# Two groups moved from DMA to TensorE transposes, DMA issues shifted between two queues, and one load issued by another engine

## The chip, the cores and the metric

One core of one Trainium2 chip (trn2) runs the whole kernel. The metric is the device time of one launch in microseconds (us); lower is better. A time is given as the median of several executions, and one execution was recorded by the hardware profiler, which is where every row below comes from.

## What is computed

The reference is one transformer block on 2048 tokens of width 128, all in float32. `mod` (six vectors of 128) is made from `c`.

```python
h = layernorm(x) * (1 + ca) + sa
q, k, v = h @ w_qkv                      # 16 heads of 64
a = softmax(causal(q k^T / 8)) v         # 2048 x 2048 per head
x = x + ga * (a @ w_out)
h = layernorm(x) * (1 + cb) + sb
e = argmax(h @ Wr.T + br)                # one of 8 experts for each token
x = x + gb * (relu(h @ W1[e].T + b1[e]) @ W2[e].T + b2[e])
```

## The kernel before

**Attention.** The 16 heads are taken as 8 pairs. A pair has 8 groups g = 0..7 of 256 queries; group g sees 2g+2 key tiles of 128 (`tiles_of`). In a group a row r = 0..3 is 128 queries of one head. TensorE (PE) makes the scores into a ring of four PSUM banks (L899). VectorE (DVE) copies them to `probs` with the row maximum (L1286, L1289, L1293). ScalarE (ACT) takes the exponential in place (L1129). Before probabilities can be multiplied by v they must be transposed, and this is done in two ways:

- *Turned on PE.* For tile j, PE transposes the four 128x128 blocks into one of three PSUM banks (L912, a "turn"), and ACT (L1137) or DVE (L1322) copies that bank to one of five slots `pT` (a "take"). The first turn of a group waits until all four rows have been through the exponential.
- *Moved by DMA.* The first `far(g)` tiles of groups 3 to 7 (4, 4, 5, 5, 5 tiles). DVE transposes within 32x32 squares into `staged` (L1303, a "shuffle", one for each row r), and small DMAs between partitions in SBUF put the squares in place in `turned_far`. Half u = 0 are rows 0 and 1, half u = 1 rows 2 and 3. A half has 16 DMAs, by a source block a = 0..3 and a target block b = 0..3. `move_blocks` (L641 to L651) issues the four of one (u, a). In the kernel before, the sync queue (SP) issues a = 0, 1 and GpSimd (POOL) issues a = 2, 3 of each half. The 8 pairs have 40 moved groups.

Then PE multiplies the turned tiles by v (L940, a "pv", one for each tile). `pv_order` puts the turned tiles first and the moved ones last. The first moved tile waits until all 32 DMAs of the group have landed. A shuffle of half u waits until the DMAs of that half of the moved group before have landed, as `staged` has one buffer.

**The order of the work.** `Plan` simulates PE, ACT and DVE step by step with written-down costs (`took`) and ready times (`ready`), and writes out one fixed order for each engine. Moves have a modelled time in `move_at`: start, then eight issues of `ISSUE` = 650 ns, then `LAND` = 4200 ns. The SP queue's order comes from `transfers`: moves, the round trip of the row sums through DRAM (L699 "put", L710 "get", which `norm` L1339 needs), weights, and the blank rows of the sorted buffer (L728). The POOL order holds moves and the copies of k to the other half of the partitions (L795). Each queue is strictly in order.

**The end.** In the last pair, as tokens are finished, PE, DVE and ACT also do the residual, the second layer norm and the routing for five parts of the tokens (4, 4, 4, 2, 2 tiles: L953, L963, L1357 to L1421, L978 to L1012). POOL scatters the rows of each tile to the sorted buffer (L803, `scatter(i)`). SP loads W2 (L693) after the last turn of group 6, and W1 (L685) and the broadcast of b2 (L686) after the last score. POOL, after `scatter(0)` to `scatter(3)`, places b1 (L813), waits for b2 and multiplies it by the gate (L818), fills small tables in the space of `staged` (L823 to L828), and issues `scatter(4)`. DVE needs these tables for `ends` (L1427), and the gated b2 before its first copy of an expert (L1458). PE turns W1 and W2 after the last pv (L1036, L1039). A loop over 23 tiles sorted by expert follows.

Of the kernel before, what the change touches and what calls it, by code (L numbers as in the profile page):

```python
# [24 lines left out]
FAR_BUFS = 2  # L25
ISSUE = 650.0
LAND = 4200.0
# [33 lines left out]
def far(g):  # L61

    return FAR.get(g, 0)


def pv_order(g):

    return list(range(far(g), tiles_of(g))) + list(range(far(g)))
# [32 lines left out]
class Plan:  # L101
# [9 lines left out]
    def __init__(self):  # L111
        groups = [(p, g) for p in range(PAIRS) for g in range(GROUPS)]
        scores = [(p, g, r, c) for p, g in groups for r in range(4) for c in range(chunks(g))]
        turns = [(p, g, j) for p, g in groups for j in range(far(g), tiles_of(g))]
        pvs = [(p, g, j) for p, g in groups for j in pv_order(g)]
        self.moves = [(p, g) for p, g in groups if far(g)]
# [43 lines left out]
        for m, (p, g) in enumerate(self.moves):  # L160
            steps += [(self.move_at(m, u)[0] + 4 * ISSUE * i, "move", (p, g, u, 2 + i)) for u in range(2) for i in range(2)]
# [19 lines left out]
    def ready(self, kind, key):  # L181
# [8 lines left out]
        if kind == "pv":  # L190
            free = 0.0
            if key[2] == pv_order(g)[0] and p + g and min(groups_of(*self.part_of(p, g))) == g:
                free = at("norm", *self.part_of(*group_before(p, g)))
            return max(self.turned_at(key), at("value", p, key[2] // 4), free)
# [7 lines left out]
        if kind == "proj":  # L202

            last = (("score", p - 1, 2 * g + 1, 3, chunks(2 * g + 1) - 1), ("score", p - 1, GROUPS - 1, 3, g),
                    ("pv", p - 1, GROUPS - 1, max(range(4 * g, 4 * g + 4), key=pv_order(GROUPS - 1).index)))[key[2]]
            return max(self.ring_free(), at(*last) if p else 0.0)
        if kind == "top":
            past = group_before(p, g, 2)
            k0, w = piece(g, key[2], key[3])
            behind = 0.0  # L210
            if past and k0 < tiles_of(past[1]) * P:
                behind = at("shuffle", past[0], past[1], key[2]) if far(past[1]) else 0.0
                over = min((k0 + w) // P, tiles_of(past[1])) - 1
                if over >= far(past[1]):
                    behind = max(behind, at("turn", past[0], past[1], over))
            return max(at("score", *key), behind)
# [7 lines left out]
        if kind == "norm":  # L224
            last = groups_of(p, g)[-1]
            i = p * CHUNKS + min(g, CHUNKS - 1) - 2
            return max([self.got(p, last), at("pv", p, last, pv_order(last)[-1])] +
# [9 lines left out]
        if kind == "wturn":  # L237
            free = max(at("pv", p, GROUPS - 1, pv_order(GROUPS - 1)[-1]),
# [14 lines left out]
    def move_at(self, m, u):  # L253

        if (m, u) not in self.moved:
            p, g = self.moves[m]
            begin = max(self.at("shuffle", p, g, 2 * u + r) for r in range(2))
            if m >= FAR_BUFS:
                q, f = self.moves[m - FAR_BUFS]
                begin = max(begin, self.at("pv", q, f, far(f) - 1))  # L260
            if u or m:
                begin = max(begin, self.move_at(m if u else m - 1, 1 - u)[0] + 8 * ISSUE)
            if begin >= NEVER:
                return NEVER, NEVER
            self.moved[m, u] = begin + HOP, begin + HOP + 8 * ISSUE + LAND
        return self.moved[m, u]

    def turned_at(self, key):

        p, g, j = key  # L270
        return self.move_at(self.move_no[p, g], 1)[1] if j < far(g) else self.at("take", *key)
# [8 lines left out]
    def transfers(self):  # L280
# [12 lines left out]
        for m, (p, g) in enumerate(self.moves):  # L293
            for u in range(2):
                for a in range(2):
# [4 lines left out]
                          self.at("shuffle", p, g - 1, 3) if far(g - 1) else 0.0) + HOP, "w2", (p,)))  # L300
# [17 lines left out]
    def took(self, kind, key, engine):  # L318
# [17 lines left out]
        if kind == "shuffle":  # L336
            return far(key[1]) * P / 0.96 + 100.0
# [43 lines left out]
    def choose_pe(self, now, soon):  # L381
# [11 lines left out]
        turn_at = place("turn", lambda k: (k[2] - far(k[1])) / float(tiles_of(k[1]) - far(k[1])))  # L393
# [23 lines left out]
def adaln_block(nc, x, w_qkv, w_out, Wr, br, W1, b1, W2, b2, c_in, wmod, out):  # L417
# [27 lines left out]
    with ExitStack() as ctx:  # L445
# [195 lines left out]
        def move_blocks(queue, key, landed):  # L641
# [4 lines left out]
            if m >= FAR_BUFS:  # L646
                q, f = plan.moves[m - FAR_BUFS]
                queue.wait_ge(pv_done, plan.order[q, f, far(f) - 1] + 1)
            for b in range(P // SQUARE):
                queue.dma_start(turned_far[b * SQUARE:(b + 1) * SQUARE, m % FAR_BUFS, u, a, 0:far(g), :],  # L650
                                staged[a * SQUARE:(a + 1) * SQUARE, u, b, 0:far(g), :]).then_inc(landed[u], 16)  # L651
# [4 lines left out]
        def _(sp):  # L656
# [21 lines left out]
            for s in plan.sp:  # L678
# [3 lines left out]
                elif s.kind == "w1":  # L682
# [3 lines left out]
                    sp.dma_start(experts[:, :, B2_AT:W2_AT],  # L686
                                 b2.rearrange("(a e) d -> a e d", a=1).broadcast_to([P, NE, E])).then_inc(b2_in, 16)
                elif s.kind == "w2":

                    sp.wait_ge(rows_turned, plan.number[p, GROUPS - 2, tiles_of(GROUPS - 2) - 1] + 1)  # L690
                    if far(GROUPS - 2):
# [38 lines left out]
            for u in range(2):  # L730
                sp.wait_ge(moved[u], 128 * len(plan.moves))
                sp.wait_ge(moved_soft[u], 128 * len(plan.moves))
# [19 lines left out]
        def _(pool):  # L752
# [59 lines left out]
            pool.wait_ge(bank_free[b_bank], b_use + 1)  # L812
            nc.gpsimd.tensor_copy(experts[:, :, B1_AT:B2_AT],  # L813
# [26 lines left out]
        def _(pe):  # L840
# [26 lines left out]
            for s in plan.pe:  # L867
# [34 lines left out]
                elif s.kind == "turn":  # L902
# [3 lines left out]
                    if j == far(g):  # L906
# [8 lines left out]
                elif s.kind == "pv":  # L915
                    j = s.key[2]
                    first, last = pv_order(g)[0], pv_order(g)[-1]
# [10 lines left out]
                    if j < far(g):  # L928
                        m_no = plan.move_no[p, g]
                        if j == 0:  # L930
                            for u in range(2):
                                pe.wait_ge(moved[u], 128 * m_no + 128)
                                pe.wait_ge(moved_soft[u], 128 * m_no + 128)
# [246 lines left out]
        def _(dve):  # L1180
# [69 lines left out]
            for s in plan.dve:  # L1250
# [17 lines left out]
                elif s.kind == "top":  # L1268
# [6 lines left out]
                    if past and far(past[1]) and c == 0:  # L1275

                        dve.wait_ge(shuffled, 4 * plan.move_no[past] + r + 1)
                    if past and k0 < tiles_of(past[1]) * P and (r == 0 or (r == 2 and c == n - 1)):

                        over = min((k0 + w) // P, tiles_of(past[1])) - 1  # L1280
                        if over >= far(past[1]):
# [13 lines left out]
                elif s.kind == "shuffle":  # L1295
# [4 lines left out]
                    if m and h == 0:  # L1300
                        dve.wait_ge(moved[u], 128 * m)
                        dve.wait_ge(moved_soft[u], 128 * m)
                    dve.transpose(staged[:, u, :, 0:far(g), h * SQUARE:(h + 1) * SQUARE],  # L1303
                                  probs[g % 2][:, r, 0:far(g) * P].rearrange("p (j b i) -> p b j i", j=far(g), i=SQUARE)
# [19 lines left out]
                elif s.kind == "norm":  # L1324
# [3 lines left out]
                    dve.wait_ge(pv_done, plan.order[p, last, pv_order(last)[-1]] + 1)  # L1328
# [190 lines left out]
```

## Time and profile before

| what | us |
|---|---|
| median of 3 executions | 979.15 |
| these executions | 978.80, 984.84, 979.15 |
| the profiled execution, its own time | 988.01 |
| its span in the profile | 986.3 |
| busy in that span: PE, DVE, ACT, POOL | 913.3, 761.9, 633.8, 422.6 |

A row of the profile names engine and line ("PE L912"), what it writes and reads (`out<-in`), how many instructions are merged (x8), when it started and how long it took, and in brackets how long the engine had been idle and what released it. SPq is the sync queue; its rows are issues of DMAs, not transfers.

### The profile page before, as it was taken

To read this page: it belongs to the slowest core of one execution; us is meant where nothing else is said; L and a number is where in the kernel's file an instruction comes from. 1 tells how busy PE (TensorE), PEld (TensorE's weight loads), DVE (VectorE), ACT (ScalarE), POOL (GpSimd) and SP (SyncE) were. 2 spreads that over 40 slices of the span, in tenths; PEclk is the share of its full clock that TensorE was granted. 3 is DMA by queue.
4 is the path that set the end of the run, shared out by engine and by line. 5 is a ranking of instruction groups with operands and counts; after the bars stand their busy time and mean duration, and the time that the engine had idled before them with its cause. 6 is when DMAs were issued, how large, how long until landed. Compare 5 with 4: busy or idle time off the path is not lost.

```text
span 986.3 us, 19842 instructions
## 1 busy us (share of the span) xinstructions
PE 913.3 (93%) x6115; PEld 674.7 (68%) x6115; DVE 761.9 (77%) x2426; ACT 633.8 (64%) x1158; POOL 422.6 (43%) x765
## 2 busy tenths in 40 slices
PE   4999999989998999899998999899989999995796
PEld 3776767667675767677676767676767666773796
DVE  6898869875997769785988599867978689971463
ACT  4876668656774768665865677577857566551574
POOL 0274515442364316542554236431745144445054
PEclk9899999999999999999999999999999999986898
DMA  2035312342144302531245214430343013372120
GB/s 81 12 91 133 100 38 64 104 125 66 29 111 109 92 23 79 136 99 47 56 106 131 66 30 113 111 95 22 88 118 87 20 47 84 87 226 69 31 67 18
DMA packets 107211, 79.13 MB, mean 80 GB/s; under 512 B 32935, under 2 KB 94163, under 8 KB 107106
## 3 DMA queue, kind: packets, MB, share of 16 engines
q1 hardware_dynamic: 85378, 51.57, 19.7%
q0 software_dynamic: 21728, 26.29, 10.2%
q8 instruction: 50, 0.82, 0.4%
q14 instruction: 55, 0.45, 0.2%
HBM read 18.21 MB, written 11.77 MB: 30 GB/s over the span
## 4 chain that ended last, share of the span: by engine, by line
PE 59%; SPq 16%; DVE 12%; issue 5%; DMA 4%; ACT 2%; another core or an unknown queue 1%; POOL 1%; POOLq 0%; DVEq 0%; ACTq 0%
PE ps L940 18%; PE ps L899 13%; SPq L650 12%; PE ps L912 12%; PE ps L878 4%; DVE probs L1286 4%; DMA turned_far<-staged 3%; PE ps L882 3%; PE ps L1064 2%; DVE probs L1289 2%; PE ps L1075 2%; PE ps L953 2%; SPq L710 2%; SPq L699 2%; DVE staged L1303 1%
## 5 line engine op out<-in xcount | busy, mean ns | idle before, releaser
L650 POOL DMA_DIRECT2D turned_far<-staged x640 | 313.1, 497 | 353.4 <-DVE staged L1303 340.4
L1129 ACT ACTIVATE probs<-probs,neg_max 128x128 f32<-128x128 f32 (+15 forms) x256 | 308.7, 1207 | 151.2 <-DVE neg_max L1293 148.6
L899 PE MATMUL ps<-k_both,q_both 128*128 128x512 f32 (+2 forms) x1280 | 344.1, 393 | 12.9 <-DVE probs L1286 7.7
L899 PEld LDWEIGHTS ps<-k_both,q_both 128*128 128x128 f32 x1280 | 208.7, 190 | 84.9 <-issue 30.5
L1286 DVE TENSOR_SCALAR_CACHE_REDUCE probs<-ps 128x512 f32<-128x512 f32 (+1 forms) x384 | 243.4, 662 | 5.0 <-PE ps L899 4.0
L1137 ACT COPY pT<-ps 128x512 f32<-128x512 f32 (+1 forms) x341 | 177.1, 557 | 94.8 <-PE ps L912 76.3
L912 PE MATMUL ps<-ident,probs 128*128 128x128 f32 x1440 | 203.8, 278 | 2.3 <-ACT probs L1129 1.4
L912 PEld LDWEIGHTS ps<-ident,probs 128*128 128x128 f32 x1440 | 172.4, 143 | 46.5 <-issue 23.3
L940 PE MATMUL ps<-pT,v_sb 128*64 128x256 f32 (+1 forms) x1568 | 179.1, 370 | 5.7 <-DVE pT L1322 3.8
L940 PEld LDWEIGHTS ps<-pT,v_sb 128*64 128x64 f32 x1568 | 104.4, 137 | 74.0 <-issue 19.1
L1303 DVE STREAM_TRANSPOSE staged<-probs 128x640 f32<-128x640 f32 (+1 forms) x160 | 122.0, 778 | 37.6 <-DMA turned_far<-staged 15.9
L1289 DVE CUSTOM_DVE_ANT_0 probs<-ps,causal 128x256 f32<-128x256 f32 (+3 forms) x256 | 130.2, 509 | 8.1 <-PE ps L899 7.8
L795 POOL CAST k_both<-k_both 64x1024 fp32r<-64x1024 f32 x64 | 66.4, 1037 | 148.2 <-DVE k_both L1265 145.6
L940 PE MATMUL ps<-turned_far,v_sb 128*64 128x256 f32 x736 | 93.0, 400 | 17.8 <-DMA turned_far<-staged 17.8
L940 PEld LDWEIGHTS ps<-turned_far,v_sb 128*64 128x64 f32 x736 | 56.1, 143 | 43.0 <-issue 24.3
L878 PE MATMUL ps<-hT,w_pair 128*128 128x512 f32 x128 | 63.4, 599 | 0.2 <-DVE q_both L1261 0.2
L1261 DVE SCALAR_TENSOR_TENSOR q_both<-ps,q_both 64x512 fp32r<-64x512 f32 x64 | 44.1, 689 | 20.9 <-ACT q_both L1115 19.7
L1322 DVE COPY pT<-ps 128x512 f32<-128x512 f32 (+1 forms) x51 | 31.5, 617 | 30.0 <-PE ps L912 15.1
L1339 DVE TENSOR_TENSOR oT<-ps,rinv_b 128x512 f32<-128x512 f32 (+1 forms) x33 | 22.1, 670 | 41.7 <-PE ps L940 40.7
L1129 ACT ACTIVATION_READ_ACCUMULATOR probs<-probs,neg_max 128x1 f32 x256 | 48.8, 190 | 0.0
L1265 DVE TENSOR_TENSOR k_both<-ps,k_both 64x512 fp32r<-64x512 f32 x64 | 44.1, 689 | 5.7 <-ACT k_both L1115 4.5
L1293 DVE TENSOR_REDUCE neg_max<-row_max 128x1 f32<-128x1 f32 (+3 forms) x256 | 39.8, 155 | 8.9
(147 smaller groups left out, 700.7 us busy)
## 6 DMA issues: line engine op xcount, KB each, us to landing
turned_far<-staged POOLq DMA_DIRECT2D x384, 40.0 KB, 2.5
turned_far<-staged SPq DMA_DIRECT2D x384, 40.0 KB, 2.0
x_sorted<-blank SPq DMA_DIRECT2D x19, 458.5 KB, 5.3
rinv_b<-spread_rows SPq DMA_DIRECT2D x128, 64.0 KB, 2.7
turned_far<-staged SPq DMA_DIRECT2D x256, 32.0 KB, 1.9
turned_far<-staged POOLq DMA_DIRECT2D x256, 32.0 KB, 1.8
spread_rows<-rinv_rows SPq DMA_DIRECT2D x256, 0.5 KB
probs<-in_L_ffn_W_dram SPq DMA_DIRECT2D x1, 2048.0 KB, 11.6
```

The source lines that it names most:

```text
L650: queue.dma_start(turned_far[b * SQUARE:(b + 1) * SQUARE, m % FAR_BUFS, u, a, 0:far(g), :], staged[a * SQUARE:(a + 1) * SQUARE, u, b, 0:fa ...
L795: nc.gpsimd.tensor_copy(k_split[h][own_half(1 - h), :, cols], k_split[h][own_half(h), :, cols]).then_inc(k_doubled[c], 1)
L878: pe.matmul(ps_ring[:, s.bank, :], w_pair[:, p % 2, j, :], hT[:, c * BANK:(c + 1) * BANK], start=True, stop=True).then_inc(bank_full[s.ban ...
L899: m = pe.matmul(ps_ring[:, s.bank, 0:w], q_split[r % 2][:, q0:q0 + P], k_split[r % 2][:, part, k0:k0 + w], start=(part == 0), stop=(part = ...
L912: m = pe.transpose(ps_turn[:, n % TURN_BANKS, P * r:P * r + P], probs[g % 2][:, r, j * P:j * P + P], ident[:])
L940: m = pe.matmul(ps_o[D * h:D * h + D, o_half + P * u0:o_half + QG], v_sb[:, j, D * h:D * h + D], of_head[:, h], start=(j == first), stop=( ...
L1129: act.activation(row, row, ACT.Exp, bias=neg_max[:, g, r:r + 1], accum_out=row_sum[:, g, r:r + 1]).then_inc(exp_done, 1)
L1137: act.copy(pT[:, n % PT_SLOTS, lo:BANK], ps_turn[:, n % TURN_BANKS, lo:BANK]).then_inc(turn_taken[n % TURN_BANKS], 1)
L1261: m = dve.scalar_tensor_tensor(out=q_split[h][own_half(1 - h), cols], in0=whole, scalar=Q_SCALE, in1=q_split[h][own_half(h), cols].bitcast ...
L1286: dve.tensor_scalar(row, ps_ring[:, bank, 0:w], 1.0, LOWEST, ALU.mult, ALU.max, accum_out=highest).then_inc(bank_free[bank], 1)
L1289: dve.tensor_tensor_reduce(row, ps_ring[:, bank, 0:w], causal[:, BANK - w:], 1.0, LOWEST, ALU.add, ALU.max, highest).then_inc(bank_free[ba ...
L1303: dve.transpose(staged[:, u, :, 0:far(g), h * SQUARE:(h + 1) * SQUARE], probs[g % 2][:, r, 0:far(g) * P].rearrange("p (j b i) -> p b j i", ...
```

## The change

- In the last pair, groups 6 and 7 have no moved tiles: `far` is 0 for the last two groups, so their 10 moved tiles are turned on PE. 38 moved groups remain.
- Of half u = 1, SP issues a = 0 only and GpSimd a = 1, 2, 3 (12 of 16). Half u = 0 stays at 8 and 8. The semaphore counts follow.
- The planner's cost of a move of half u = 1 is 12 issues of 500 ns instead of 8 of 650 ns, and the order of POOL's moves is by 500 ns. The whole plan is made anew with this.
- The broadcast load of b2 is issued by GpSimd after `scatter(3)`, not by SP behind W1.

```diff
+LAST_NEAR = 2
+HARD, SOFT = (128, 64), (128, 192)
 ISSUE = 650.0
+SOFT_ISSUE = 500.0
...
-def far(g):
-    return FAR.get(g, 0)
+def far(p, g):
+    return FAR.get(g, 0) if p * GROUPS + g < PAIRS * GROUPS - LAST_NEAR else 0
...
-            steps += [(self.move_at(m, u)[0] + 4 * ISSUE * i, "move", (p, g, u, 2 + i)) for u in range(2) for i in range(2)]
+            steps += [(self.move_at(m, u)[0] + 4 * SOFT_ISSUE * i, "move", (p, g, u, 2 - u + i)) for u in range(2) for i in range(2 + u)]
...
             if u or m:
-                begin = max(begin, self.move_at(m if u else m - 1, 1 - u)[0] + 8 * ISSUE)
+                begin = max(begin, self.move_at(m if u else m - 1, 1 - u)[0] + (12 * SOFT_ISSUE, 8 * ISSUE)[u])
...
-            self.moved[m, u] = begin + HOP, begin + HOP + 8 * ISSUE + LAND
+            self.moved[m, u] = begin + HOP, begin + HOP + (8 * ISSUE, 12 * SOFT_ISSUE)[u] + LAND
...
-                for a in range(2):
+                for a in range(2 - u):
                     steps.append((self.move_at(m, u)[0] + 4 * ISSUE * a, "move", (p, g, u, a)))
...
                     sp.dma_start(w1_rows[:], W1.rearrange("e (f p) d -> p (e f) d", p=P)).then_inc(w1_in, 16)
-                    sp.dma_start(experts[:, :, B2_AT:W2_AT],
-                                 b2.rearrange("(a e) d -> a e d", a=1).broadcast_to([P, NE, E])).then_inc(b2_in, 16)
...
             b_bank, b_use = plan.bank_of("small", 0, 0)
             pool.wait_ge(bank_free[b_bank], b_use + 1)
+            pool.dma_start(experts[:, :, B2_AT:W2_AT],
+                           b2.rearrange("(a e) d -> a e d", a=1).broadcast_to([P, NE, E])).then_inc(b2_in, 16)
             nc.gpsimd.tensor_copy(experts[:, :, B1_AT:B2_AT],
```

Elsewhere `far(g)` and `pv_order(g)` become `far(p, g)` and `pv_order(p, g)`, and the waits on `moved` and `moved_soft` count 128 and 64, and 128 and 192, for each moved group.

## Rows read from the trace of the kernel before

**Rows 1.** Busy time of each engine in a stretch, granted PE clock, DMA share, GB/s

```profile
631.00:736.00 105.00, 101.77 (x684) 73.34 (x684) 85.88 (x259) 72.16 (x126) 47.33 (x88) 1.00 0.31 82
...
850.00:912.00 62.00, 49.75 (x311) 36.61 (x310) 34.82 (x133) 23.70 (x35) 32.32 (x53) 0.81 0.48 139
...
880.00:885.00 5.00, 5.00 (x31) 4.61 (x33) 3.31 (x19) 1.17 (x2) 4.61 (x9) 0.66 1.04 358
```

**Rows 2.** Waits of the whole run: who waited for whom, us in total, times, longest

```profile
PE ps L940 <- DMA turned_far<-staged: 17.8, 13, 3.5
...
DVE staged L1303 <- DMA turned_far<-staged: 15.9, 9, 2.7
...
PE ps L899 <- DVE probs L1286: 7.7, 9, 1.0
```

**Rows 3.** Chain that ended last, in order of time: moved tiles of group 5

```profile
204.08 4.07 PE ps L940 x20
...
526.30 2.38 PE ps L940 x20
...
736.36 2.36 PE ps L940 x20
```

**Rows 4.** Moves: issue ns min/median/max on each queue; KB and median us to landing

```profile
L650 SPq DMA_DIRECT2D turned_far<-staged x640: 507/591/1766, 49.5 to 893.5; - x160
L650 POOL DMA_DIRECT2D turned_far<-staged x640: 496/496/742, 49.8 to 883.1; - x160
...
turned_far<-staged POOLq DMA_DIRECT2D x384, 40.0 KB, 2.5
turned_far<-staged SPq DMA_DIRECT2D x384, 40.0 KB, 2.0
```

**Rows 5.** Timelines of DVE, POOL, SP and PE round the moves of group 5

```profile
617.73 1.57 DVE L1303 STREAM_TRANSPOSE staged<-probs 128x640 f32<-128x640 f32 x2 [2.72 <-DMA turned_far<-staged]
...
619.59 3.91 POOL L650 DMA_DIRECT2D turned_far<-staged  x8 [6.57 <-DVE staged L1303]
...
623.00 0.60 SPq L728 DMA_DIRECT2D x_sorted<-blank  x1
623.70 10.61 SPq L650 DMA_DIRECT2D turned_far<-staged  x16
...
631.35 2.38 PE L940 MATMUL ps<-turned_far,v_sb 128*64 128x256 f32 x20 [1.36 <-DMA turned_far<-staged]
```

**Rows 6.** Chain that ended last, last pair: two turns, then eight pvs

```profile
857.74 0.87 PE ps L912 x8
...
862.56 3.60 PE ps L940 x32
```

**Rows 7.** Timelines of PE, ACT and DVE in the last group's end

```profile
876.28 2.57 PE L912 MATMUL ps<-ident,probs 128*128 128x128 f32 x12 [0.53 <-ACT probs L1129]
...
905.05 4.54 PE L940 MATMUL ps<-turned_far,v_sb 128*64 128x256 f32 x20
...
894.15 0.56 ACT L1144 ACTIVATE hT<-ps,mod 128x256 f32<-128x256 f32 x1 [7.53 <-issue]
901.54 0.86 ACT L1137 COPY pT<-ps 128x512 f32<-128x512 f32 x2 [6.83 <-remote]
...
899.38 0.69 DVE L1322 COPY pT<-ps 128x512 f32<-128x512 f32 x1 [14.68 <-remote]
...
921.73 0.29 DVE L1427 TENSOR_TENSOR staged<-ps,staged 128x128 f32<-128x128 f32 x1 [0.27 <-PE ps L1022]
```

**Rows 8.** Timelines of SP and POOL in the same stretch

```profile
876.18 7.43 SPq L686 DMA_DIRECT2D experts<-in_L_ffn_b_dram  x1
...
891.63 2.47 SPq L650 DMA_DIRECT2D turned_far<-staged  x4
...
905.89 0.96 POOL L803 DMA_INDIRECT x_sorted<-x_sb,slot  x1 [7.07 <-DVE slot L1415]
...
908.44 2.35 POOL L818 TENSOR_TENSOR experts<-experts,gate_b 128x1024 f32<-128x1024 f32 x1
```

More of the change, by code:

```diff
@@ L113, in __init__ @@
         scores = [(p, g, r, c) for p, g in groups for r in range(4) for c in range(chunks(g))]
-        turns = [(p, g, j) for p, g in groups for j in range(far(g), tiles_of(g))]
-        pvs = [(p, g, j) for p, g in groups for j in pv_order(g)]
-        self.moves = [(p, g) for p, g in groups if far(g)]
+        turns = [(p, g, j) for p, g in groups for j in range(far(p, g), tiles_of(g))]
+        pvs = [(p, g, j) for p, g in groups for j in pv_order(p, g)]
+        self.moves = [(p, g) for p, g in groups if far(p, g)]
         shuffles = [(p, g, r) for p, g in self.moves for r in range(4)]
@@ L211, in ready @@
             if past and k0 < tiles_of(past[1]) * P:
-                behind = at("shuffle", past[0], past[1], key[2]) if far(past[1]) else 0.0
+                behind = at("shuffle", past[0], past[1], key[2]) if far(*past) else 0.0
                 over = min((k0 + w) // P, tiles_of(past[1])) - 1
-                if over >= far(past[1]):
+                if over >= far(*past):
                     behind = max(behind, at("turn", past[0], past[1], over))
@@ L237, in ready @@
         if kind == "wturn":
-            free = max(at("pv", p, GROUPS - 1, pv_order(GROUPS - 1)[-1]),
+            free = max(at("pv", p, GROUPS - 1, pv_order(p, GROUPS - 1)[-1]),
                        at("turn", p, GROUPS - 2, tiles_of(GROUPS - 2) - 1) + W_LAND,
@@ L270, in turned_at @@
         p, g, j = key
-        return self.move_at(self.move_no[p, g], 1)[1] if j < far(g) else self.at("take", *key)
+        return self.move_at(self.move_no[p, g], 1)[1] if j < far(p, g) else self.at("take", *key)
     def part_of(self, p, g):
@@ L336, in took @@
         if kind == "shuffle":
-            return far(key[1]) * P / 0.96 + 100.0
+            return far(*key[:2]) * P / 0.96 + 100.0
         if kind == "top":
@@ L730, in _ @@
             for u in range(2):
-                sp.wait_ge(moved[u], 128 * len(plan.moves))
-                sp.wait_ge(moved_soft[u], 128 * len(plan.moves))
+                sp.wait_ge(moved[u], HARD[u] * len(plan.moves))
+                sp.wait_ge(moved_soft[u], SOFT[u] * len(plan.moves))
             sp.wait_ge(chosen_known, 1)
@@ L916, in _ @@
                     j = s.key[2]
-                    first, last = pv_order(g)[0], pv_order(g)[-1]
+                    first, last = pv_order(p, g)[0], pv_order(p, g)[-1]
                     part = plan.part_of(p, g)
@@ L1327, in _ @@
                     last = groups_of(p, c)[-1]
-                    dve.wait_ge(pv_done, plan.order[p, last, pv_order(last)[-1]] + 1)
+                    dve.wait_ge(pv_done, plan.order[p, last, pv_order(p, last)[-1]] + 1)
                     part = p * NC + first // TPC
```

44 lines of the change are left out of this document (22 added, 22 removed).

## The prediction

> **What bounds the kernel now.** I read the share of each engine by stretch first, then the waits, then the chain of waits, and last the timelines at two places. In a late full pair PE is busy 101.77 of 105.00 us and DVE 85.88 [rows 1]: PE bounds the pair, and no more than 3.2 us of a pair are idle on it. The list of waits says which idle time hangs on the moves: 17.8 us of PE before the first moved tile, 15.9 us of DVE before a shuffle (its buffer is still being read by DMAs), and 7.7 us of PE waiting for DVE's copies of scores, some of which were late because of such a shuffle [rows 2]. That is 25 us of PE time at most over the whole run. The second place is the end of the last pair: from 850 to 912 us PE is busy only 49.75 of 62 us, at a granted clock of 0.81 of 2.4 GHz [rows 1].
>
> **The execution and the median.** The profiled execution took 988.01 us, the median is 979.15. The same point of a pair (moved tiles of group 5) comes at 204.08, 526.30 and 736.36 [rows 3]: three pairs took 322.2 us (107.4 each), the next two 210.1 (105.0 each). Had the first three been like the later ones, the profiled time would be 7.1 us lower, 980.9. So I take the late pairs as the picture of a median execution, work out what is saved against them, and subtract it from 979.15.
>
> **Part 1: four issues of each second half go from SP to POOL.** SP needs a median of 591 ns for an issue and POOL 496 [rows 4]. With 38 moved groups SP issues 38 x 12 = 456 moves instead of 640, POOL 38 x 20 = 760 instead of 640. Group 5 of a pair shows what it does [rows 5]. DVE's two shuffles of the second half end at 619.3. POOL begins at 619.59 and needs 3.91 for its eight. SP comes to them only at 623.70, behind other work of its queue (the row at 623.00 is a load of blank rows), and needs 10.61/16 = 0.66 us for each: eight are issued at 629.0, and with 2.0 us to landing [rows 4] that is 631.0. PE starts at 631.35 after waiting 1.36. After the change SP's four are issued at 626.4 and landed at 628.4; POOL's twelve are issued at 619.59 + 12 x 0.49 = 625.5 and landed 2.5 us later, at 628.0. PE was ready at 630.0, so its wait goes, with 1.6 us to spare, and SP's backlog is 2.6 us shorter for each group, so that also DVE's 2.72 us before the shuffle at 617.73 [rows 5] shrinks. Where SP is not behind, it is the other way round: POOL's twelve land 12 x 0.497 + 2.5 = 8.5 us after the shuffle, while SP's eight took 8 x 0.591 + 2.0 = 6.7. This 1.8 us costs nothing only while PE has other work in hand, and the planner now reckons 12 x 500 + 4200 = 10.2 us for such a half, more than the 8.5.
> Bounds: nothing is gained if the next wait (ACT's exponential, DVE's copies) ends as late; at most the 3.2 us of a pair. Group 5's wait and part of the one us of PE behind DVE are what the rows show, so I take 1.5 us a pair. Over the seven pairs that go from the first into the last (the early groups of a pair have no moves and the first pair's start is not like the others): 10 us. Range 0 to 22.
>
> Beside this stands a rule of the Trainium skill that speaks against giving POOL more: by "SBUF — State Buffer" (the part on the shared port pair), a DVE instruction in a two-port mode keeps GpSimd from writing DMA descriptors, and an issue of about 620 ns can become one of 3100. The row disagrees for this mix of instructions: 640 issues on POOL took 496, 496 and 742 ns (min, median, max) [rows 4]. By the rule the sum would lose this term; by the row nothing changes.
>
> **Part 2: groups 6 and 7 of the last pair turned on PE.** Added: 10 turns. Two turns are 0.87 us in the chain [rows 6], so 10 x 0.435 = 4.4 us of PE at full clock, and ten more copies by ACT and DVE, of some 0.6 to 0.7 us each ([rows 7]: 0.69 on DVE), which lie beside PE's next turns. Removed: 8 shuffles on DVE (1.57 us for two, [rows 5], 6.3 us in all), 32 issues on SP and 32 on POOL, and 64 x 40.0 KB = 2.6 MB of DMA traffic [rows 4]. No wait of PE for these moves stands in the list near the end, so what counts is what else the traffic does. From 880 to 885 us the DMA engines are busy at 1.04 of their time [rows 1]: W2, W1, b2 and the moves of group 7 come together. Just then two engines stop for reasons that no row explains: ACT idles 7.53 us ("issue") and again 6.83 ("remote"), DVE 14.68 ("remote"), up to 899.38 and 901.54 [rows 7], although PE had turned their tiles. PE stands still with them and then does the last moved tiles at half clock: 4.54 us at 905.05 [rows 7] for what takes 2.36 at full clock [rows 3]. I estimate that this stall is a consequence of the traffic (it sits right behind the full stretch), without being able to show it. The change takes group 7's 32 moves (1.3 MB), and b2 out of it.
> Sum: PE's idle time from 850 to 912 is 12.25 us [rows 1]. If all but 2 of it goes, and the half clock of the last pvs (2.2 us), against 4.4 of turns, the last pv ends 10.25 + 2.2 - 4.4 = 8 us earlier. Ends: if all the idle time goes, 10 us; if none, -4 (a loss). I take 8.
>
> **Part 3: b2 issued by POOL.** SP loses an issue of 7.43 us, behind which its last four moves stood until 891.63 + 2.47 [rows 8]. Those moves are gone, so it is worth nothing by itself; the row sums of group 7 get free, which the last norm needs only at the last pv. On POOL b2 now comes behind `scatter(3)`, which waited for DVE until 905.89 [rows 8]: two scatters of 0.96 with a gap, 2.3 us; the issue d; landing 2.5 (a move's, [rows 4]); the product 2.35 [rows 8]. Behind it in POOL's queue stand the tables that DVE needs at 921.73 [rows 7], and the last scatter. So 921.73 - 905.89 - 2.3 - 2.5 - 2.35 = 8.7 us are free for d, less up to 1 for the tables. The trace has no such issue on POOL: the nearest is a move, 0.5 us for 32 partitions [rows 4]. Between 0.5 (an issue is an issue), 2.0 (by partitions, 128 against 32) and 15.9 (by contiguous pieces, 128 x 8 against 32) I take 2.0, as the scatter row with its 128 rows costs 0.96: hidden, 0 us. By the last, 15.9 - 7.7 = 8 us late. The opposite sign is excluded: nobody waits for b2 before 926.
>
> **Sum.** 979.15 - 10 - 8 + 0 = 961 us. Everything after the last pv (some 77 us) stays as it is.
>
> **The rivals.**
> *The stall stays* (22%). The idle time of ACT and DVE outlasts the full stretch, which speaks against traffic as its cause. Then Part 2 costs 4 us: 979.15 - 10 + 4 = 973.
> *PE-bound pairs give nothing* (11%). The saved waits come back as waits for DVE or as a new order's gaps: 979.15 - 8 = 971.
> *b2 late* (8%). An issue of 15.9 us: 961 + 8 = 969.
> *POOL becomes the late mover* (7%), the case on the other side. In each place where PE or DVE waits for moves today, POOL's twelve issues decide: 13 waits of PE [rows 2] grow by 1.8 us, 23 us in all, and the 10 of Part 1 are not gained: 979.15 + 23 - 8 = 994. It decides from the point where SP was less than 1.8 us behind when the shuffles ended. For it: POOL's queue also holds the k copies in strict order. Against it: in rows 5 SP was 4 us behind, and the planner knows of 12 x 500.
> The forecast holds 52%; its own range is 953 to 969.
>
> **Range and chances.** Three of the four rivals lie between 969 and 973; the order of all engines is made anew, which I allow 4 us each way. 952 to 979 leaves out some 2 in 10. A measurement of this kernel can tell about 1% from no change: under 969.4 or over 988.9. Under 969.4 are nearly all of the forecast (0.50), a fifth of the first rival, and about 0.4 of the second and third: 0.62. Over 988.9 is the last rival, 0.07. Within 1%: 0.31.
>
> **What would show it.** Right for Part 1: PE's wait for moved tiles falls from 17.8 to under 6 us, DVE's before shuffles under 8, a pair is 103 to 104 us with the same busy time. For Part 2: no idle stretch over 3 us of ACT and DVE before the last pv, which ends at most 12 us after the last group's exponential chain, and a PE clock above 0.9 there. For Part 3: POOL's issue of b2 under 3 us, and DVE at L1427 released by PE, not by POOL. Wrong: pairs still at 105 with waits under another name; the stall in place; DVE at L1427 waiting for POOL; PE's wait for moved tiles longer than 17.8.

## The result, and the profile after

| | median of runs, us | n | against before |
|---|---|---|---|
| before, beside it | 982.0 (978.8 to 985.66) | 4 | |
| changed kernel | 941.39 (939.77 to 942.2) | 4 | ratio 0.9583 [0.9537, 0.9629] |
| its profiled execution | 942.05, span 940.3 | | |

The change takes 41 us; 18 were forecast, and 941.39 lies outside the range 952 to 979. Medians here are of all executions, ratios of the fast ones alone (one of ten of `near_only` and three of twelve of `b2_only`, below, were slow), so a ratio is not quite the quotient of two medians. The sign and the places were right, both gains are at least twice what I gave them, and one part that was to cost nothing costs 4.4 us.

The first view answers to [rows 1]: shares by stretch (span, then busy time of PE, PE's weight loads, DVE, ACT, POOL; clock, DMA share, GB/s), cut at the same instruction of each pair, a run of 24 pvs of 2.34 us in the chain of waits. The second is the same for the kernel before, cut at the same instruction. Lines of the changed kernel are those of before plus 3 (the pvs are L943, the scores L902, the moves L653).

```profile
137.94:238.94 101.00, 100.70 (x686) 72.96 (x688) 84.46 (x258) 72.55 (x129) 57.07 (x108) 1.00 0.35 88
...
339.85:442.73 102.88, 100.79 (x686) 72.82 (x688) 84.28 (x258) 72.55 (x129) 57.06 (x108) 1.00 0.35 87
...
644.51:745.38 100.87, 100.56 (x687) 72.92 (x688) 84.35 (x258) 72.56 (x129) 57.16 (x108) 1.00 0.30 78
745.38:857.60 112.22, 107.14 (x751) 79.98 (x751) 92.57 (x360) 66.07 (x108) 48.16 (x80) 0.98 0.28 84
...
868.00:878.00 10.00, 10.00 (x48) 10.00 (x49) 4.16 (x20) 2.19 (x4) 2.02 (x2) 0.50 0.05 14
```

```profile
142.44:250.71 108.27, 103.41 (x686) 74.32 (x688) 85.93 (x260) 72.10 (x127) 47.29 (x88) 0.98 0.32 83
...
676.29:781.31 105.02, 101.79 (x687) 73.35 (x688) 85.89 (x260) 72.16 (x127) 47.33 (x88) 1.00 0.28 75
781.31:909.60 128.29, 112.17 (x711) 81.05 (x712) 96.37 (x366) 62.50 (x100) 58.12 (x100) 0.90 0.35 99
909.60:986.30 76.70, 61.36 (x511) 59.63 (x511) 38.51 (x134) 43.71 (x132) 26.41 (x31) 0.90 0.14 37
```

Between the two spans lie 46.0 us, in four places:

- up to the first cut: 142.44 - 137.94 = 4.5;
- six pairs: 638.9 against 607.4, 31.4. By pair it is 7.3, 7.8, 2.5, 5.5, 4.1 and 4.1. A pair is now 100.9 with PE idle for 0.3; the one of 102.88 has a wait of 1.8 for POOL's copy of k, which stands behind moves;
- from there to the last pv: 128.3 against 112.2, 16.1. PE's idle time falls by 11.0 (16.1 to 5.1), and its busy time by 5.0 although it does ten turns more, at a granted clock of 0.98 instead of 0.90;
- after the last pv: 76.7 against 940.3 - 857.6 = 82.7, a loss of 6.0. PE runs there for 10 us at half clock (0.50 at 868 to 878).

In the list of waits PE's wait for moved tiles is gone (17.8 in [rows 2]), and DVE's before a shuffle is 0.4 (15.9). At group 5 ([rows 5]) the timelines of POOL, SP and PE now show:

```profile
590.00 9.76 POOL L653 DMA_DIRECT2D turned_far<-staged  x20 [3.10 <-DVE staged L1306]
...
591.81 0.61 SPq L729 DMA_DIRECT2D x_sorted<-blank  x1
592.51 8.15 SPq L653 DMA_DIRECT2D turned_far<-staged  x12
...
603.83 2.38 PE L943 MATMUL ps<-turned_far,v_sb 128*64 128x256 f32 x20
```

POOL issues 20 in a run, SP ends at 600.66, 3.2 before PE wants the tiles, and PE comes to them without a wait.

The median of before is itself uncertain by more than the 7 us that I argued about: in the runs that stood beside the experiments it was 984 to 988 (976 to 996 in single runs), while each variant with the new split stays within 5 us. Differences below therefore go by ratios, or between variants that have the split. The changed kernel was not run again beside those variants: a difference to its 941.39 is one between sessions.

### The profile page after: what moved, and what is told of

Its sections match the earlier page's. It is cut to its first block, busy times and chain, and to the rows that moved or that the text cites. A ratio compares the mean times of both kernels' runs of the same rounds, so it can differ in the third digit from the quotient of the medians.

```text
span 940.3 us, 19844 instructions
## 1 busy us (share of the span) xinstructions
PE 900.3 (96%) x6155; PEld 672.1 (71%) x6155; DVE 750.0 (80%) x2407; ACT 640.0 (68%) x1179; POOL 482.2 (51%) x886
## 4 chain that ended last, share of the span: by engine, by line
PE 84%; DVE 10%; issue 2%; ACT 1%; POOL 1%; DMA 0%; DVEq 0%; POOLq 0%; SPq 0%; ACTq 0%
PE ps L943 25%; PE ps L902 24%; PE ps L915 17%; PE ps L881 5%; PE ps L885 3%; DVE probs L1289 3%; PE ps L1067 2%; PE ps L956 2%; PE ps L1078 2%; DVE probs L1292 1%; PE ps L1042 1%; POOL turned_far L653 1%; ACT probs L1132 1%; DVE accT L1353 1%; DVE oT L1342 1%
## 5 line engine op out<-in xcount | busy, mean ns | idle before, releaser
L653 POOL DMA_DIRECT2D turned_far<-staged x760 | 371.5, 497 | 230.1 <-DVE staged L1306 201.0
L902 PE MATMUL ps<-k_both,q_both 128*128 128x512 f32 (+2 forms) x1280 | 345.0, 392 | 8.2 <-DVE q_both L1264 2.0
L902 PEld LDWEIGHTS ps<-k_both,q_both 128*128 128x128 f32 x1280 | 207.3, 190 | 75.1 <-issue 28.9
L1140 ACT COPY pT<-ps 128x512 f32<-128x512 f32 (+1 forms) x362 | 185.8, 559 | 97.6 <-PE ps L915 80.0
L915 PEld LDWEIGHTS ps<-ident,probs 128*128 128x128 f32 x1480 | 176.3, 141 | 45.1 <-issue 25.7
L915 PE MATMUL ps<-ident,probs 128*128 128x128 f32 x1480 | 207.9, 275 | 0.6 <-ACT probs L1132 0.5
L943 PE MATMUL ps<-pT,v_sb 128*64 128x256 f32 (+1 forms) x1608 | 180.2, 367 | 0.5 <-ACT pT L1140 0.5
L943 PEld LDWEIGHTS ps<-pT,v_sb 128*64 128x64 f32 x1608 | 107.3, 136 | 64.2 <-issue 17.7
L1306 DVE STREAM_TRANSPOSE staged<-probs 128x640 f32<-128x640 f32 (+1 forms) x152 | 114.7, 773 | 3.5 <-ACT probs L1132 2.4
L943 PE MATMUL ps<-turned_far,v_sb 128*64 128x256 f32 x696 | 82.8, 383 | 0.0
L943 PEld LDWEIGHTS ps<-turned_far,v_sb 128*64 128x64 f32 x696 | 47.4, 137 | 23.8 <-issue 4.1
L1118 ACT ACTIVATE q_both<-ps 64x512 fp32r<-64x512 f32 x64 | 37.8, 590 | 10.6 <-PE ps L881 10.1
L1325 DVE COPY pT<-ps 128x512 f32<-128x512 f32 (+1 forms) x40 | 23.3, 596 | 26.2 <-PE ps L915 24.8
```

Of the source, the lines that this page charges most:

```text
L902: m = pe.matmul(ps_ring[:, s.bank, 0:w], q_split[r % 2][:, q0:q0 + P], k_split[r % 2][:, part, k0:k0 + w], start=(part == 0), stop=(part = ...
L915: m = pe.transpose(ps_turn[:, n % TURN_BANKS, P * r:P * r + P], probs[g % 2][:, r, j * P:j * P + P], ident[:])
L943: m = pe.matmul(ps_o[D * h:D * h + D, o_half + P * u0:o_half + QG], v_sb[:, j, D * h:D * h + D], of_head[:, h], start=(j == first), stop=( ...
L1140: act.copy(pT[:, n % PT_SLOTS, lo:BANK], ps_turn[:, n % TURN_BANKS, lo:BANK]).then_inc(turn_taken[n % TURN_BANKS], 1)
L1306: dve.transpose(staged[:, u, :, 0:far(p, g), h * SQUARE:(h + 1) * SQUARE], probs[g % 2][:, r, 0:far(p, g) * P].rearrange("p (j b i) -> p b ...
```

## The experiments

### Which part gives what

Four kernels, each with one part of the change; b2 stays on SP in all four.

**`split_only`**: the split and its planner costs, no tiles turned in the last groups.

```diff
-LAST_NEAR = 2
+LAST_NEAR = 0
```

> Only the 12 of 16 split and the planner's new cost of it; groups 6 and 7 of the last pair keep their moves, b2 stays on SP. Theory 1 (the backlog of SP's issues is what made a pair long): full pairs fall from 105-108.7 us to about 101, as in the changed kernel, so some 32 us less than before, ratio about 0.967. Theory 2 (most of the gain came from the end of the last pair): pairs stay near 105, ratio above 0.985.

Measured: 957.32 (4 runs), ratio 0.9747 [0.9698, 0.9796]. The pairs are those of the changed kernel (100.9 to 101.0, one of 102.9), as theory 1 has it. The gain is smaller than its 32 us because the rest, from the last full pair's cut at 745.54, takes 208.9 us where before took 205.0: the stall shown below is there, and longer.

**`split_old_costs`**: the same, with the planner's figures of before, so that PE, DVE and ACT have the order of before and only the two queues differ.

```diff
-begin = max(begin, ...move_at(...)[0] + (12 * SOFT_ISSUE, 8 * ISSUE)[u])
+begin = max(begin, ...move_at(...)[0] + 8 * ISSUE)
```

> The same split of the issues, but the planner's costs of before (8 issues of 650 ns for either half), so PE, ACT and DVE have the order of the kernel before. Theory 1 (it is the queues): pairs of 101 to 102 us, ratio about 0.97, within 0.5% of the run with the new costs. Theory 3 (it is the new order of PE, ACT and DVE that puts moved tiles later): most of the gain is missing, ratio above 0.985.

Measured: 957.74 (4 runs), 0.9751 [0.9699, 0.9804].

**`costs_only`**: the new planner figures with the old 8 and 8 issues.

```diff
-LAST_NEAR = 2
+LAST_NEAR = 0
-HARD, SOFT = (128, 64), (128, 192)
+HARD, SOFT = (128, 128), (128, 128)
```

> Issues stay 8 and 8 in each half; only the planner's cost of a second half is the new one (12 x 500 ns in place of 8 x 650), so the order alone is new. Theory 1: no change beyond 1% (ratio 0.99 to 1.01), PE's wait for moved tiles stays over 12 us. Theory 3: ratio about 0.97, PE's wait for moved tiles near 0.

Measured: 974.04 (8 runs), 0.9897 [0.9853, 0.994]. Its pairs are 102.7 to 105.6 long. Neither theory had the waits right: PE's wait for moved tiles is down to 0.9 us and DVE's before a shuffle to 2.6, but PE's wait for DVE's copies of scores is up from 7.7 to 14.8. With the old queues the new order mostly gives the wait another name. From its list of waits:

```profile
PE ps L902 <- DVE probs L1289: 14.8, 8, 2.9
...
PE ps L943 <- DMA turned_far<-staged: 0.9, 2, 0.5
```

**`near_only`**: groups 6 and 7 of the last pair on PE, with the split and the figures of before.

```diff
-HARD, SOFT = (128, 64), (128, 192)
+HARD, SOFT = (128, 128), (128, 128)
 LAST_NEAR = 2
...
-begin = max(begin, ...move_at(...)[0] + (12 * SOFT_ISSUE, 8 * ISSUE)[u])
+begin = max(begin, ...move_at(...)[0] + 8 * ISSUE)
```

> Only groups 6 and 7 of the last pair are turned on PE; split 8 and 8, costs and b2 as before. If the moves' share of the DMA traffic caused the stall of ACT and DVE of before (up to 901.5 us): no idle of ACT or DVE over 3 us before the last pv, ratio 0.985 to 0.99 (10 to 14 us less). If W1, W2 and b2 alone cause it: the stall stays, ratio 1.00 or a little above.

Measured: 985.34 (10 runs), 1.0001 [0.9967, 1.0035].

What follows. The split is worth 2.5%, by the queues alone: the same order of instructions, run with other queues, gives all of it. The pair of `split_old_costs`, in the view by stretch, against the 105.0 of [rows 1]:

```profile
345.16:446.67 101.51, 101.09 (x686) 72.50 (x688) 85.68 (x260) 72.14 (x127) 57.03 (x108) 1.00 0.34 88
```

The new figures add 0.6 us in a late pair (101.5 to 100.9), which the end of that run gives back (208.9 against 204.6). With the old queues the figures alone are worth 1%. Groups 6 and 7 on PE alone give nothing that ten runs can tell (within 0.4%). In the trace the last stage is 6.8 us shorter (198.2 against 205.0 from the last full pair's cut), but its pairs were 105.0 to 109.3 long in that execution, and it meets the lock shown below.

### What stops ACT and DVE in the last group

My theory of the prediction was DMA traffic. The trace of `split_only` speaks against it: ACT stands still for 14.40 us up to 871.75 and DVE for 11.69 up to 868.92, both "remote", while the DMA share is 0.17, not 1.04. The first fence is the share by stretch, the second the timelines of POOL, DVE and ACT.

```profile
857.00:863.00 6.00, 3.78 (x34) 2.27 (x32) 0.23 (x1) 0.35 (x1) 4.56 (x5) 1.00 0.17 56
863.00:871.50 8.50, 2.08 (x6) 1.39 (x6) 0.42 (x1) 0.00 (x0) 6.37 (x8) 0.62 0.17 54
```

```profile
854.59 1.05 POOL L806 DMA_INDIRECT x_sorted<-x_sb,slot  x1 [0.30 <-issue]
...
871.11 0.95 POOL L806 DMA_INDIRECT x_sorted<-x_sb,slot  x1 [0.30 <-issue]
...
868.92 0.42 DVE L1342 TENSOR_TENSOR oT<-ps,rinv_b 128x256 f32<-128x256 f32 x1 [11.69 <-remote]
...
871.75 0.59 ACT L1154 COPY experts<-ps 128x512 f32<-128x512 f32 x1 [14.40 <-remote]
```

What fits is POOL: 14 scatters, one every 1.26 us from 854.59 to 872.1, queued up behind its moves. The kernel before has 12 in a row up to 898.8, and DVE goes on at 899.38 [rows 7]. The changed kernel has no moves there, POOL comes to the scatters as they fall due, in bursts of 4, 4, 4 and 2, and no wait "remote" is left. (The last two scatters follow at 874.3.) So the new theory: a long run of queued scatters holds ACT and DVE up; the traffic does not. Four kernels tell them apart.

**`after_scatter_late`**: the changed kernel, its scatters held back until three parts are ready. No moves run beside them.

```diff
             pool.wait_ge(blanked, 16 * len(plan.blanks))
+            pool.wait_ge(slots_ready, 3)
```

> The changed kernel with one more wait: POOL starts scatter(0) only when the slots of part 2 are known, so 12 scatters come back to back from about 842 us, with no moves near them. Theory S: ACT and DVE stop for 5 to 12 us until the burst ends at about 857, and the kernel takes 948 to 955 us. Theory T: nothing depends on the scatters there, 941 to 943 us.

Measured: 950.81 (4 runs), 0.9641 [0.9598, 0.9684]: 9.4 us above the changed kernel. POOL issues 12 scatters from 840.96 to 855.9. Share by stretch, and the timelines of ACT, DVE and PE:

```profile
852.00:858.00 6.00, 0.27 (x4) 0.18 (x2) 0.00 (x0) 0.00 (x0) 3.01 (x4) 0.78 0.23 72
```

```profile
858.21 0.56 ACT L1148 ACTIVATE hT<-ps,mod 128x256 f32<-128x256 f32 x1 [8.01 <-remote]
...
858.26 0.69 DVE L1326 COPY pT<-ps 128x512 f32<-128x512 f32 x1 [11.15 <-remote]
...
858.82 1.02 PE L997 MATMUL ps<-wrT,hT 128*128 128x8 f32 x4 [6.55 <-ACT hT L1148]
```

Bunching the scatters brings the stall back, without one move in the stretch. The last pv ends 13.1 us later than in the changed kernel (870.77 against 857.62); of these the time loses only 9.4, because here POOL's product of b2 is all but over when the last layer norm comes, which it holds up in the changed kernel (next section).

**`after_scatter_fours`**: the same hold, but POOL waits for the landing of each four before it issues the next.

```diff
+                    if t and t % 4 == 0:
+                        pool.wait_ge(scattered, 16 * t)
                     pool.indirect_dma_start(x_sorted, ...)
```

> As after_scatter_late (12 scatters from about 841 us), but POOL waits after every four until these have landed, so that at most four are under way. Theory S1 (what holds ACT and DVE up is the number of scatters under way or queued): no idle of ACT or DVE with releaser 'remote' over 1.5 us, 941 to 945 us instead of 950.8; what is left over 941.4 is that b2 and its product come some 6 us later. Theory S2 (it is that POOL issues scatters at all while ACT and DVE work there): they stop again, 950 us or more.

Measured: 942.72 (4 runs), 0.9539 [0.9481, 0.9598]. The same 14 scatters, held back as long (842.35 to 868.9), at most four under way: the longest "remote" is 1.4 us, the last pv ends only 0.7 us later than in the changed kernel, and the time loses 1.3 instead of 9.4. So it is not that POOL scatters while ACT and DVE work there. The waits for landing do two things at once, though: they keep the number under way at four, and they put 2 to 6 us without an issue between the fours. Which of the two matters was not separated.

**`before_scatter_early`**: the kernel before, with the scatters placed between POOL's moves as each part gets ready.

```diff
+        steps += [(self.at("slots", PAIRS - 1, i), "scatter", (PAIRS - 1, i)) for i in range(2)]
```

> The kernel before, but POOL issues scatter(0) and scatter(1) as soon as their slots are known, between the moves of the last pair, so that no more than 4 to 6 scatters stand back to back; all moves and the loads of W1, W2 and b2 stay. Theory S (a burst of about 12 scatters on POOL holds up ACT and DVE): no idle of ACT or DVE over 3 us with releaser 'remote' or 'issue' round the last group; the stretch from 781 us to the end is some 8 to 12 us shorter than before, ratio 0.985 to 0.99. Theory T (the DMA traffic of moves and weights holds them up, my forecast's reason): the stall of 7 and 14 us stays, ratio 1.00.

Measured: 981.71 (10 runs), 0.9969 [0.9933, 1.0005]. The stall of ACT and DVE is gone, as theory S says, but not the 8 to 12 us: from the last full pair's cut the trace is 6.3 us shorter (198.7 against 205.0), and the time hardly changes. Timelines of SP and PE:

```profile
875.79 7.34 SPq L687 DMA_DIRECT2D experts<-in_L_ffn_b_dram  x1
...
890.75 2.46 SPq L651 DMA_DIRECT2D turned_far<-staged  x4
...
895.81 3.80 PE L946 MATMUL ps<-turned_far,v_sb 128*64 128x256 f32 x20 [7.06 <-DMA turned_far<-staged]
```

PE now stands 7.06 us for group 7's moved tiles, which SP issues last behind b2 (7.34) and the row sums. In the kernel before SP's last moves were issued as late (894.1 us, [rows 8]), and the stall lasted longer, so this wait lay under it: taking the stall away shows the wait.

**`far_scatter_early`**: the changed kernel with all its moves back, scatters placed early, b2 on POOL, and the product of b2 behind the last layer norm.

```diff
-LAST_NEAR = 2
+LAST_NEAR = 0
+        steps += [(self.at("slots", PAIRS - 1, i), "scatter", (PAIRS - 1, i)) for i in range(2)]
```

> The 12 of 16 split with groups 6 and 7 of the last pair still moved by DMA, scatter(0) and scatter(1) issued between the moves, b2 issued by POOL, product by the gate after the last layer norm. Theory Q (turning the last two groups on PE paid because it took the moves out of the way of the scatters and of b2's issue, not because PE's turns are cheap): 937 to 943 us, within 1% of the changed kernel. If it is the DMA traffic of the moves beside W1 and W2 that matters: ACT, DVE or PE stop for over 5 us near the last group and it takes 948 us or more.

Measured: 945.73 (4 runs), 0.957 [0.9511, 0.9628], between the two forecasts. ACT and DVE still lose 5.9 and 5.8 ("remote") behind 12 moves and 6 scatters of POOL in a row.

What follows. `split_only` to `after_b2_sp` (below) is 957.32 to 937.03: with the split in, turning groups 6 and 7 on PE gives 20.3 us. More than half of that is to be had with the moves still there: from `split_only` to `far_scatter_early`, 11.6 us go by POOL's work alone (its order of scatters and product, and b2 issued there and not by SP), and a milder stall stays. Against `after_gate_later` (936.28, below), which has the same place for the product and no moves in these groups, 9.4 are left for the turning itself.

### b2 and its product

**`after_b2_sp`**: the changed kernel, b2 issued by SP again.

```diff
                     sp.dma_start(w1_rows[:], W1...)
+                    sp.dma_start(experts[:, :, B2_AT:W2_AT], b2...).then_inc(b2_in, 16)
...
-            pool.dma_start(experts[:, :, B2_AT:W2_AT], b2...).then_inc(b2_in, 16)
```

> The changed kernel with b2 issued by SP behind W1 again. My forecast counts the move of b2 as 0: within 1 us of the changed kernel, 940 to 943. If the 5 to 7 us that SP's issue of b2 takes delays W2 or the row sums of the last group (which come behind it on SP), it is 2 to 6 us slower.

Measured: 937.03 (6 runs), 0.95 [0.9467, 0.9533]: 4.4 us below the changed kernel, which neither forecast had. The slowest of its runs (938.6) is faster than the fastest of the changed kernel (939.77).

**`b2_only`**: the kernel before with only b2 moved to POOL.

```diff
-                    sp.dma_start(experts[:, :, B2_AT:W2_AT], b2...).then_inc(b2_in, 16)
...
+            pool.dma_start(experts[:, :, B2_AT:W2_AT], b2...).then_inc(b2_in, 16)
```

> The kernel before with b2 issued by POOL after scatter(3). SP's last four moves no longer stand behind its 7.4 us, but the burst of 12 scatters behind POOL's moves stays, and with it the stall of ACT and DVE until about 900 us. So little is gained: ratio 0.995 to 1.00; if DVE is held up by POOL's product in the last layer norm as in the changed kernel, up to 5 us worse: 1.005.

Measured: 989.63 (12 runs), 0.9996 [0.9955, 1.0036]. Two things happen in its trace: the product starts at 910.89 and meets DVE's layer norm (an operation of 0.16 us takes 2.22, PE waits 2.05), and the stall is broken up: ACT has waits of 4.64 and 5.32, DVE of 6.63 and 4.55, all "remote", round the same 12 scatters, where before had 7.53 and 6.83, and 14.68. In sum they are hardly shorter.

**`after_gate_later`**: the changed kernel, with the product (L821) placed after the tables and behind the last layer norm.

```diff
+            pool.wait_ge(norm_ready, NC + len(parts_of(PAIRS - 1)))
             pool.wait_ge(b2_in, 16)
             ...
             nc.gpsimd.tensor_tensor(b2_b, b2_b, gate_b[:]..., ALU.mult).then_inc(b2_gated, 1)
```

> The changed kernel, but POOL fills its tables first and multiplies b2 by the gate only after DVE has finished the last second layer norm (a wait on norm_ready). Theory P (DVE's 2.35 us for an instruction of 0.16 us at 861.24 is POOL's 2.37 us product holding the port that both use; PE then idles 2.2 us and its clock falls to half from 868 to 878): that instruction is back at 0.16 us, PE's clock stays at full speed, and 4 to 7 us go: 935 to 937 us. Otherwise: unchanged within 1 us, or later by the product's 2.4 us if POOL's tables or scatter come late.

Measured: 936.28 (6 runs), 0.9491 [0.9459, 0.9524]. This is the fastest version of the study, 5.1 us below the changed kernel; `after_b2_sp`, at 937.03, cannot be told from it. Timelines of POOL, DVE and PE of the changed kernel:

```profile
856.44 0.95 POOL L814 DMA_DIRECT2D experts<-in_L_ffn_b_dram  x1
...
861.19 2.37 POOL L821 TENSOR_TENSOR experts<-experts,gate_b 128x1024 f32<-128x1024 f32 x1 [3.54 <-DMA experts<-in_L_ffn_b_dram]
...
861.24 2.35 DVE L1374 TENSOR_SCALAR var<-mean_var 128x2 f32<-128x2 f32 x1
...
866.48 0.44 PE L981 MATMUL ps<-ident,accT 128*128 128x128 f32 x2 [2.21 <-DVE accT L1387]
...
874.62 4.55 PE L1042 MATMUL ps<-gate_diag,probs 128*128 128x128 f32 x24
...
881.00 0.50 DVE L1461 COPY probs<-experts 128x644 f32 x1 [3.09 <-issue]
```

and of `after_gate_later` (one line further down in the code):

```profile
861.38 0.16 DVE L1375 TENSOR_SCALAR var<-mean_var 128x2 f32<-128x2 f32 x1
...
864.43 2.36 POOL L831 TENSOR_TENSOR experts<-experts,gate_b 128x1024 f32<-128x1024 f32 x1 [5.92 <-DVE accT L1388]
...
869.29 2.92 PE L1043 MATMUL ps<-gate_diag,probs 128*128 128x128 f32 x24
...
874.03 0.50 DVE L1462 COPY probs<-experts 128x644 f32 x1 [1.46 <-issue]
```

An operation of DVE on 128x2 numbers, 0.16 us long, takes 2.35 when it starts 0.05 after POOL's product, and both end at 863.6. The layer norm is on the path: PE waits 2.21 us with nothing to do. Then the granted clock falls to 0.50 from 868 to 878, and 24 transposes of W2 take 4.55 instead of 2.92. The first copies of an expert, which need all of W2, start at 881.00 instead of 874.03. Of those 7.0 us some 2.1 are the lock (L981 at 866.48 against 864.40), and the rest is PE at half clock. Both kernels then have one more stretch at half clock, behind PE's wait of 5.0 to 5.5 us for the first expert: 882 to 888 in the changed kernel, 877 to 884 in this one. The lock adds a stretch to that one. With b2 on SP the product runs at 856.67, before that layer norm, and nothing meets it. In `near_only` POOL comes to its product at 909.22, right behind its scatters, and the lock and the clock are the same (timeline of DVE, then share by stretch); 4 us of the kernel before, where the product ran at 908.44 while DVE had nothing to do, stand below:

```profile
909.33 2.28 DVE L1377 TENSOR_SCALAR rough<-var 128x2 int32<-128x2 int32 x1
```

```profile
914.00:918.00 4.00, 3.72 (x18) 3.73 (x19) 0.55 (x4) 1.15 (x2) 0.00 (x0) 0.56 0.00 0
```

```profile
915.00:919.00 4.00, 4.00 (x36) 3.81 (x35) 1.80 (x10) 2.92 (x6) 0.00 (x0) 1.00 0.01 4
```

The three kernels with the lock (changed, `near_only`, `b2_only`) have a clock of 0.50 to 0.57 behind it; the three without (before, `after_b2_sp`, `after_gate_later`) have 1.00 at that place (and 0.93 and 0.94 from 868 to 878 as a whole, which holds the start of the other stretch). So the lock, and PE's wait of 2.05 to 2.21 us behind it, bring the half clock here. The length of the wait alone does not decide it: in `far_scatter_early` PE waits 2.64 us up to 863.62, and the clock stays at 1.00 until 878. What makes the difference is open. The row, from its timeline of PE:

```profile
863.62 0.70 PE L963 MATMUL ps<-oT,wo_pair 128*128 128x256 f32 x2 [2.64 <-DVE oT L1349]
```

Here the trace agrees with the Trainium skill: by "SBUF — State Buffer" (SBUF: two separate sides), GpSimd and a DVE operation that wants the port pair they share exclude each other for a whole instruction, and 2.35 against 0.16 us is such a case (in two other kernels 2.28 and 2.22). Not every DVE operation is held up: in `after_scatter_late` the product runs from 872.33 to 874.71 beside the addition from PSUM and the two batch norm operations of the last layer norm, which keep their 0.42, 0.49 and 0.25 us, and only the copy behind them is stretched, from 0.17 to 0.42. The same section's other case, issues of moves on POOL stretched beside DVE, did not show here either: 760 issues had 496, 496 and 742 ns, as in [rows 4].

### How far the split can go

**`both_halves`**: the changed kernel with 12 of 16 issues on POOL in both halves.

```diff
-HARD, SOFT = (128, 64), (128, 192)
+HARD, SOFT = (64, 64), (192, 192)
```

> The changed kernel with 12 of 16 issues on POOL in both halves. POOL then has 24 issues (11.7 us) and the copies of k for a group of 11 to 13 us. If POOL is then the late mover (the rival on the slow side of my forecast): PE waits for moved tiles over 10 us in all, pairs of 103 us or more, 955 us or more. If only the sum of both queues matters: 941 to 944 us.

The planner's cost is 12 issues of 500 ns for either half here, so the order of PE, DVE and ACT is a new one too.

Measured: 974.0 (4 runs), 0.9858 [0.9797, 0.9918]: 32.6 us above the changed kernel. The pairs are 105.8 to 108.2 long. Waits of the whole run, then POOL's timeline in one pair:

```profile
DVE staged L1306 <- DMA turned_far<-staged: 22.2, 11, 4.2
...
PE ps L902 <- DVE probs L1289: 15.6, 8, 3.3
```

```profile
694.53 19.52 POOL L653 DMA_DIRECT2D turned_far<-staged  x40 [2.36 <-issue]
```

POOL issues 40 moves in a run: at 24 a group it is the late mover, while at 20 it ends with SP (599.8 and 600.7 at group 5 above). The sign that was expected is missing, though: PE's wait for moved tiles is not in the list at all, where over 10 us were forecast. The lateness shows as DVE's wait before shuffles (22.2) and PE's wait for DVE's copies (15.6). No run has these queues with the old order, so how much of the 32.6 is the order's is not shown.

## Why the prediction was right or wrong

**Part 1, 10 us forecast.** Right: the place (SP behind in its queue, POOL idle), the 1.36 us of PE at group 5 gone, DVE's 15.9 down to 0.4, and that POOL's queue holds 20 issues a group. Mis-sized: the term of 10 us measured some 25 (the split alone, 2.5%), and the traces of before and after lie 35.9 us apart up to the last full pair. Three steps failed:

- "at most the 3.2 us of a pair". The late pair fell by 4.15, of which 2.9 is idle time (3.2 to 0.3) and 1.2 is PE's *busy* time (101.77 to 100.56), with the same 687 matmuls at the same clock. Of the 1.2, 0.7 comes with the order of before (`split_old_costs`: 101.09), the rest with the new one. So busy time holds waits, and it was no floor. The Trainium skill warns of this measure in "Perfetto Trace Analysis" (Identifying the Most-Contended Engine): matmul busy time says little about how near a kernel is to its limit, as pipelined matmuls look smaller in a trace, and the share of peak arithmetic and the weight loads' busy time are to be used. Here the weight loads had 73.34 of 105.00, and I didn't weigh it; no run shows how much of that gap can be had.
- "so I take 1.5 us a pair", where the bound was 3.2. Nearly every wait behind a late move went, not only group 5's and part of one more: the rows of waits had shown 25 us, and I counted 10 of them.
- "I take the late pairs as the picture of a median execution". They weren't: other medians of before are 982 to 988, and pairs of 104 to 110 come up in every trace with the old queues and the old order. They are what the split ends.

**Part 2, 8 us forecast.** In the two traces the last pv comes 16.1 us earlier, counted from the last cut; and with the split in place the part gives 20.3. The stall was the right thing to look at, and it went altogether; its cause was wrong. "I estimate that this stall is a consequence of the traffic" failed: 14.40 us of it stand at a DMA share of 0.17, and 12 queued scatters alone bring it back. The rival's evidence, that the idle time outlasts the full stretch, was the better reading. The ten turns, 4.4 us, did not show as a loss: from the last full pair's cut to the last pv PE's busy time fell by 5.0 in spite of them, at a clock of 0.98 instead of 0.90. The sum had allowed 2.2 us for the clock. "PE clock above 0.9" held up to the last pv (0.98).

**Part 3, 0 us forecast.** The issue on POOL takes 0.95 us, less than the 2.0 assumed, and DVE at L1430 waits for PE and not for POOL, as forecast. It costs 4.4 us all the same: I counted when the product would be done, but not what it does to DVE while it runs. The step that failed is "Everything after the last pv (some 77 us) stays as it is": 82.7. The rule of the shared ports was weighed at POOL's issues, where no row shows an effect, and not at POOL's product, where it decides. (The 620 and 3100 ns that the prediction has from the Trainium skill, "SBUF — State Buffer", are there times of a whole DMA issued by GpSimd and not of its issue.)

**The rivals.** *The stall stays*, *the pairs give nothing*: no. *b2 late*: late neither by 8 us nor in that way. *POOL the late mover*: not at 20 issues a group; at 24 POOL is late, but PE's waits for moved tiles, on which the rival's 33 us (961 to 994) rested, do not come, so the 32.6 measured there agree with it by chance. 4 us each way for a new order was too little: with the new queues `split_old_costs` and `split_only` differ by 0.4, with the old ones the new order is worth 10 (`costs_only`, 974.04 against 984.48 of before beside it). The parts sum: 25 + 20.3 - 4.4 = 41, but only in this order: the 20.3 hold the stall that is longer in `split_only` than before. Alone, the second and the third give nothing.

## What to carry to other kernels

PE's busy time is no floor. Waits behind a late queue can be worth their whole sum in the list of waits and more (25 us listed, some 25 gained); but a wait that goes from the list may only have changed its name, so look at the length of the stage. Where two engines stop together with an unexplained releaser, look at what the third one issues just then and test that alone; a stall can cover a second wait of the same length. An operation that is moved in time must be counted for what it locks in its new place, not only for when it ends.

## What was not expected of the hardware

- 12 to 14 indirect DMAs that GpSimd issues one after another stop ACT and DVE for 8 to 19 us in all (the longest is ACT's 18.7 in `split_old_costs`), at a DMA share of 0.17 to 0.23 where it was read. The kernel before and `b2_only` let them go on for a moment in between. Eight cost 4.3 us (`near_only`: DVE idle up to 862.47, the last scatter issued at 861.48), four none. They go on between 3.2 us before the end of the burst (DVE in `split_only`) and 2.7 behind it (ACT in the kernel before). How the two engines hang on that queue is open. Loading of their instructions does not explain it as far as the traces show: in `after_scatter_late` one packet of the instruction queue starts at 848.6 and none from 850 to 862, while both engines stand until 858.2, and `after_scatter_fours` has such a packet at the same time and no stall.
- b2 as 1024 pieces of 512 bytes takes 0.95 us to issue on POOL and 4.8 to 7.43 on the sync queue, behind W1.
- A wait of 2.2 us of PE cost some 5 more up to the first copy of an expert, and some 4 up to the end of the trace (940.3 against 934.4), through the granted clock: 0.50 from 868 to 878, in which PE was never idle. A wait of 2.64 us in `far_scatter_early` cost no clock.
